# Four graph layers on one core: in the last layer TensorE reads the features in place, the first store is queued later, and the ending is cut in two

## The reference

```python
h = jnp.maximum(_layernorm(x, axis=-1), 0.0)
support = h @ weight
mask = (adj != 0)
rank = jnp.cumsum(mask, axis=1)
deg = rank[:, -1:]
k = jnp.minimum(deg, 100.0)
pos = rank - (deg - k)
w = mask * jnp.where(pos > 0, 0.5 ** (k - pos), 0.0)
x = x + w @ support + bias
```

## Time and profile before

| | before |
|---|---|
| median of 3 runs | 1181.51 us (1181.3 to 1183.08) |
| the profiled execution | 1179.22 us |
| its span in the profile | 1177.5 us |
| PE busy | 1082.3 us (92%) |
| DVE, ACT, POOL busy | 869.1, 769.3, 265.1 us |
| PE's mean granted clock | 0.956 of full speed |

### The profile page before, as it was taken

The page is one execution under the profiler, slowest core; times in us unless marked ns, Lnnn a source line. Parts: engine busy times, 40 slices in busy tenths (PEclk is TensorE's granted clock), DMA queues, the critical chain, the costliest instruction groups (busy, mean ns, idle before and its releaser), DMA issues.

```text
span 1177.5 us, 14630 instructions
## 1 busy us (share of the span) xinstructions
PE 1082.3 (92%) x5065; PEld 502.5 (43%) x5084; DVE 869.1 (74%) x927; ACT 769.3 (65%) x791; POOL 265.1 (23%) x183
## 2 busy tenths in 40 slices
PE   4899999996599999999898999999999999936987
PEld 1233333346533333333343545555555454534555
DVE  7999989965856666886689777767676777676543
ACT  3455555543566666866777798777778888535864
POOL 3110000000100000000143644333334444423533
PEclk9999999996889999999798999999999999967999
DMA  8999999950068888888344355545453554202652
GB/s 314 404 381 357 351 325 363 352 201 1 1 218 284 286 283 259 277 282 269 128 135 151 90 168 172 176 147 176 149 174 119 185 161 126 89 0 71 204 181 80
DMA packets 96301, 238.19 MB, mean 202 GB/s; under 512 B 16368, under 2 KB 45040, under 8 KB 79856
## 3 DMA queue, kind: packets, MB, share of 16 engines
q1 hardware_dynamic: 87024, 220.62, 56.4%
q10 hardware_dynamic: 9216, 16.78, 3.7%
HBM read 219.55 MB, written 17.83 MB: 202 GB/s over the span
## 4 chain that ended last, share of the span: by engine, by line
PE 75%; DVE 14%; issue 5%; ACT 5%; DMA 1%; POOL 1%; SPq 0%; DVEq 0%; ACTq 0%; POOLq 0%
PE PS L453 48%; PE PS L659 9%; PE PS L597 5%; PE PS L598 4%; PE PS L687 4%; DVE TB L1149 3%; PE PS L485 1%; PE PS L475 1%; ACT work L882 1%; PE PS L463 1%; PE PS L711 1%; ACT work L785 1%; DVE work L1428 1%; DVE work L1422 1%; ACT work L956 1%
## 5 line engine op out<-in xcount | busy, mean ns | idle before, releaser
L412 POOL TENSOR_TENSOR ring<-work,ring 128x1024 f32<-128x1024 f32 x58 | 139.2, 2400 | 474.7 <-DVE work L1428 474.7
L1275 DVE TENSOR_TENSOR work<-work,ring 128x1024 f32<-128x1024 f32 x128 | 151.2, 1222 | 75.3 <-ACT work L882 75.0
L819 ACT ACTIVATE work<-PS 128x1024 uint8<-128x1024 f32 x128 | 124.1, 1021 | 118.5 <-PE PS L453 118.5
L882 ACT ACTIVATE work<-PS,att_sc 128x1024 f32<-128x1024 f32 x128 | 147.7, 1202 | 78.6 <-PE PS L598 71.2
L453 PE MATMUL PS<-ring,work 128*65 128x256 f32 (+1 forms) x592 | 189.3, 467 | 6.4 <-DVE work L1452 2.8
L453 PE MATMUL PS<-work 128*64 128x512 f32 (+1 forms) x656 | 168.7, 559 | 0.1
L1422 DVE SCALAR_TENSOR_TENSOR work<-PS,work 128x1024 f32<-128x1024 f32 x72 | 88.1, 1223 | 90.6 <-PE PS L453 77.4
L659 PE MATMUL PS<-TB,TA 65*128 65x512 f32 x288 | 141.0, 612 | 3.5 <-DVE work L1422 3.5
L453 PEld LDWEIGHTS PS<-ring,work 128*65 128x65 f32 x592 | 80.4, 138 | 92.2 <-issue 69.1
L961 ACT ACTIVATE work<-work 128x1024 f32<-128x1024 f32 x72 | 76.0, 1055 | 43.7 <-DVE work L1422 43.6
L597 PE MATMUL PS<-work 128*128 128x512 f16 x256 | 99.0, 387 | 4.8 <-DVE work L1098 3.1
(11 more groups left out here) (211 smaller groups left out, 1511.5 us busy)
## 6 DMA issues: line engine op xcount, KB each, us to landing
ring<-in_adj_t SPq DMA_DIRECT2D x96, 1024.0 KB, 5.3
ring<-in_adj_t SPq DMA_DIRECT2D x103, 512.0 KB, 4.1
work<-in_adj_t SPq DMA_DIRECT2D x32, 1024.0 KB, 7.9
codes<-work ACTq DMA_DIRECT2D x64, 256.0 KB, 7.0
ring<-codes SPq DMA_DIRECT2D x64, 256.0 KB, 3.1
H<-in_adj_t SPq DMA_DIRECT2D x25, 512.0 KB, 4.0
X<-in_x SPq DMA_DIRECT2D x2, 512.0 KB, 5.2
out_x<-X SPq DMA_DIRECT2D x2, 512.0 KB, 4.4
```

What stands on the lines that cost most here:

```text
L412: nc.gpsimd.tensor_tensor(near(n), sums(n), near(n), ALU.mult).then_inc(sem("near_ready"), 1)
L819: nc.scalar.activation(made[:, k, u * UNIT:(u + 1) * UNIT], PS[:, (4 + 2 * u) * BANK:(6 + 2 * u) * BANK], ACT.Relu).then_inc(sem("codes_ma ...
L882: nc.scalar.activation(att[:, u, :], PS[:, (4 + 2 * u) * BANK:(6 + 2 * u) * BANK], ACT.Sigmoid, bias=att_sc[:, 2:3], scale=att_sc[:, 1:2]) ...
L1275: V.tensor_tensor(prob[:, m % 4, :], att[:, u, :], ring[:, s % RING, u * UNIT:(u + 1) * UNIT], ALU.mult)\
```

## The change

1. PE reads its stationary operand from `S3` itself. `sstage`, POOL's 64 copies and the semaphore `staged3` are gone. PE waits for `parts3_ready` 1 ahead of step 0 of each half's first group and for 2 ahead of step 16, where it waited for 2 ahead of the first.
2. As the address in `S3` differs in each step, PE's 56 looped steps are written out.
3. `store(0)` goes behind all loads of codes in SP's queue.
4. At the end ACT copies the first 512 columns of the sums and DVE the other 512; PE turns and DVE adds each part apart, and each is stored by a transfer of its own (`store_quarter`).

```diff
+            def store_quarter(a):
+                t = TG + a * TG // 2
+                sp.wait_ge(sem("quarter_ready"), a + 1)
+                sp.dma_start(out_nodes[:, t:t + TG // 2], X[:, t:t + TG // 2]).then_inc(sem("stored"), 16)
...
-                if h:
-                    store(0)
...
-            store(1)
-            sp.wait_ge(sem("stored"), 16 * G)
+            store(0)
+            for a in range(2):
+                store_quarter(a)
+            sp.wait_ge(sem("stored"), 16 * 3)
...
-            pool.wait_ge(sem("parts3_ready"), 1)
-            for h in range(2):
-                for k in range(4):
-                    if h:
-                        pool.wait_ge(sem("agg3_done"), h * T + k - 4 + 1)
-                    nc.gpsimd.tensor_copy(sstage[:, k, :].rearrange("p (s c) -> p s c", s=3), S3[:, k, :, :])\
-                      .then_inc(sem("staged3"), 1)
...
             def to_nodes(rhs, at, dst, b=None):
                 for a in range(2):
-                    if b is not None:
-                        bias_rows(b, dst + a)
-                    for q in range(4):
...
+                    ins = to_nodes_bank(rhs, at, dst, a, b)
+                return ins
+
+            def to_nodes_bank(rhs, at, dst, a, b=None):
...
-            pe.wait_ge(sem("parts3_ready"), G)
 
             def step3(h, s, k, first=False):
 
-                pe.wait_ge(sem("staged3"), s + 1)
+                if s in (0, TG):
+                    pe.wait_ge(sem("parts3_ready"), 1 + s // TG)
...
-                            ins = add(PS[D * c:D * c + D, b * BANK:(b + 1) * BANK], sstage[:, k, part * D:(part + 1) * D],
+                            ins = add(PS[D * c:D * c + D, b * BANK:(b + 1) * BANK], S3[:, s % T, part, :],
...
-                with pe.Fori(1, T // 4) as it:
-                    for k in range(4):
-                        step3(h, it * 4 + (h * T + k), k)
-            pe.wait_ge(sem("sums_out3_v"), 1)
-            to_nodes(ident[:, :], UNIT, 2).then_inc(sem("agg3_nodes"), 1)
+                for n in range(4, T):
+                    step3(h, h * T + n, n % 4)
+            for a in range(2):
+                pe.wait_ge(sem("sums_out3_v" if a else "sums_out3_a"), 1 if a else 2)
+                to_nodes_bank(ident[:, :], UNIT, 2, a).then_inc(sem("agg3_nodes"), 1)
...
+            one("sums_out3_a", TA[:, UNIT:UNIT + BANK], banks(6, 7), ACT.Copy, ("agg3_done", 2 * T))
...
-            copy_out("sums_out3_v", TA[:, UNIT:2 * UNIT], PS[:, 6 * BANK:8 * BANK], ("agg3_done", 2 * T))
-            result(1)
+            copy_out("sums_out3_v", TA[:, UNIT + BANK:2 * UNIT], banks(7, 8), ("agg3_done", 2 * T))
+            dve.wait_ge(sem("bias3_added"), G)
+            for a in range(2):
+                t = TG + a * TG // 2
+                dve.wait_ge(sem("agg3_nodes"), 2 + a)
+                V.tensor_tensor(X[:, t:t + TG // 2], X[:, t:t + TG // 2],
+                                banks(2 + a, 3 + a).rearrange("p (t c) -> p t c", c=D), ALU.add).then_inc(sem("quarter_ready"), 1)
```

More of the change, by code:

```diff
@@ L138, in graph_layers @@
         st = [sb(f"st{k}", [P, T]) for k in range(10)]
-        sstage = sb("sstage", [P, 4, 3 * D], BF16)
         kmask = sb("kmask", [P, 1])
@@ L431, in _ @@
                   .then_inc(sem("bias3_added"), 1)
-            pool.wait_ge(sem("parts3_ready"), 1)
-            for h in range(2):
-                for k in range(4):
-                    if h:
-                        pool.wait_ge(sem("agg3_done"), h * T + k - 4 + 1)
-                    nc.gpsimd.tensor_copy(sstage[:, k, :].rearrange("p (s c) -> p s c", s=3), S3[:, k, :, :])\
-                      .then_inc(sem("staged3"), 1)
-                pool.wait_ge(sem("parts3_ready"), G)
-                with pool.Fori(1, T // 4) as it:
-                    for k in range(4):
-                        pool.wait_ge(sem("agg3_done"), it * 4 + (h * T + k - 4 + 1))
-                        nc.gpsimd.tensor_copy(sstage[:, k, :].rearrange("p (s c) -> p s c", s=3), S3[:, it * 4 + k, :, :])\
-                          .then_inc(sem("staged3"), 1)
         @block.tensor
@@ L458, in to_nodes @@
                 for a in range(2):
-                    if b is not None:
-                        bias_rows(b, dst + a)
-                    for q in range(4):
-                        o = banks(dst + a, dst + a + 1).rearrange("p (r b c) -> p b r c", r=2, b=4)
-                        ins = mm(o[:, q, :, :], TA[:, at + a * BANK + q * P:at + a * BANK + (q + 1) * P], rhs,
-                                 start=b is None, stop=True, skip_group_check=True)
+                    ins = to_nodes_bank(rhs, at, dst, a, b)
+                return ins
+            def to_nodes_bank(rhs, at, dst, a, b=None):
+                if b is not None:
+                    bias_rows(b, dst + a)
+                for q in range(4):
+                    o = banks(dst + a, dst + a + 1).rearrange("p (r b c) -> p b r c", r=2, b=4)
+                    ins = mm(o[:, q, :, :], TA[:, at + a * BANK + q * P:at + a * BANK + (q + 1) * P], rhs,
+                             start=b is None, stop=True, skip_group_check=True)
                 return ins
```

## The result

| | before | after |
|---|---|---|
| median | 1182.3 us (1181.3 to 1183.83, 4 runs) | 1173.74 us (1173.37 to 1173.83, 4 runs) |
| ratio | | 0.9926 (0.9909 to 0.9943) |
| the profiled execution, its span | 1179.22, 1177.5 us | 1173.66, 1171.9 us |

The change made the kernel 8.6 us faster by the medians and 5.6 us by the profiled executions.

The account below looks back on a forecast made before the run. PE's matmul rate was taken to bound most of the fourth layer, with losses at start, turn and end. 1.0 + 2.95 + 2.3 = 6.25 us, with 0.65 for the clock, takes 1181.5 to 1174.6 us; range 1171.8 to 1178.0.

Parts of the forecast that it names:

- The start (1.0): Fourth layer's first steps: PE waits for one DVE sum, not two; 1.2 us earlier, some lost to half clock, gain 1.0.
- The turn (2.95): Between the halves in the fourth layer: PE's whole 2.95 us stall goes once the store no longer delays loads of codes.
- the cover: At the turn: power 40 is ready near 1131.5, PE needs it at 1134.40; 2.9 us of cover, so no new wait.
- Unrolling (0): PE's looped steps in the fourth layer: writing them out gains or costs 0 us, with 5 more code packets.
- Rival (e): PE's written-out steps: PE catches up with its own code and waits for packets; 17 us slower, 1198.6 us; chance 0.04.
- The end (2.3): After the last step: copies, turns and sums in halves give 1.2 us, bytes 1.2 less 0.1 for overlap; gain 2.3.
- The term of the bytes, 1.2 - 0.1: Last store: only 256 KB remains last, saving 1.2 us of byte time, less 0.1 where the two transfers meet.
- The last bytes flow for 2.4 us again: At the final stores: a sign that the prediction is wrong, byte flow still lasting 2.4 us.
- Rival (d): Final stores: the two are served one behind the other, end gains 0.5, total 5.1 us, 1176.4 us; chance 0.04.
- The clock's allowance (0.65): Turn of the halves: the stall may cost other executions a 1.3 us slow stretch; half, 0.65, added for the median.
- Rival (b): Clock doesn't fall ahead of the first steps, or fell mostly at the turn: gain 8.9 us, 1172.6 us; chance 0.14.
- theory C: From the experiments: the gain's rest is TensorE's clock, often falling in the kernel before's stall at the turn.

Follow-up runs that it names:

- after_again: The changed kernel timed once more, unaltered: ratio 0.9917 to the kernel before, mean 1173.0 us.
- unroll_only: The kernel before with only PE's 56 looped steps written out, POOL still staging: ratio 0.9986.
- store_only: The kernel before with only the first store moved behind the loads of codes: ratio 0.9970, mean 1177.3 us.
- one_store: The changed kernel with the last half stored by one 512 KB transfer after both sums: ratio 0.9938, mean 1175.5 us.
- direct_only: The kernel before with PE reading S3 itself, steps written out and the early start; store and ending as before: ratio 0.9980, mean 1179.2 us.
- store_in_place: The changed kernel with the first store put back between the loads: ratio 0.9962 to the kernel before, mean 1178.1 us.
- b_again: The kernel before timed once more, unaltered: ratio 1.0002.
- end_only: The kernel before with only the ending cut in two: ratio 0.9988, mean 1180.0 us.
- stall_busy: The changed kernel with the first store back between the loads and 12 unread matmuls in the resulting stall: ratio 0.9948, mean 1177.1 us.
- late_start: The changed kernel with PE waiting for both sums of the feature parts ahead of step 0: ratio 0.9942, mean 1175.8 us.

## Why the prediction was right, by its own steps

The sum of 6.25 us for the profiled execution came out: 6.24 from the first flip to the end with the same hold (`before` and `after_again`). The profile of the result showed 5.6, the 6.7 of the table less the 1.1 by which its flip was late; that both lie near 6.25 is partly chance. Term by term, with `after_again` for like and like:

| term | forecast | result's profile | `after_again` |
|---|---|---|---|
| start | 1.0 | 1.52 | 1.12 |
| turn | 2.95 | 3.15 | 3.15 |
| end | 2.3 | 2.01 | 1.96 |

**The start (1.0)** was on the path as said. The first sum gave 1.2, the pause behind the two sums shrank from 0.29 to 0.04, which I had left out though its row stood there, and 0.3 went back to the slow time, as worked out. The result's profile shows 0.4 more because its linear map was that much shorter, which comes with the early hold. What I missed is that with the late start the slow time can last longer: 49.63 and 49.76 us in two of the six profiles whose first step waits for both sums, 48.16 or 48.17 in the other four. The two are just those with the early hold, in which the linear map took 4.29 and 4.28 us and not 4.69 or 4.70. With the early start and idle PE it is 48.50 in all six, with either hold. Why the hold and the start decide it together stays open.

**The turn (2.95)** gave 3.15, and the cover held: with the store gone from between the loads, alone or with the rest, PE had no wait there.

**Unrolling (0)** is not told from nothing: the ratio of `unroll_only` (0.9971 to 1.0002) allows a gain of up to 3.4 us, but the rows leave no room for one. 28 steps take 36.40 us looped (`store_only`) and written out (`after`), the longest wait of the matmuls without a releaser is still 0.2 us after the change, and q8 has 4 packets more (5 estimated). Rival (e) falls.

**The end (2.3)** gave 2.0, but not in the way that I had said. Copies, turns and sums took as the rows of half the size said: 0.60, 2.07 and 0.69; that is the 1.2 us which remain when `one_store` is taken off. The term of the bytes, 1.2 - 0.1, had the mechanism wrong. I had the first quarter's bytes nearly through when the second's begin, so that 1.2 us of bytes are left. In fact the bytes begin 0.9 us after the issue of the first store (1167.71 to 1168.6; before, 1173.27 to 1174.2), which is when the second is issued, and then all 512 KB flow in one stream of 2.4 us. "The last bytes flow for 2.4 us again" was one of my signs of being wrong, and it came true. What the two transfers give is that the same stream starts earlier: 0.1 us behind the last sum's end at 1168.51, where it was 1.0 behind it before. That is worth the 0.83 us of `one_store`, near the estimated 1.1 by luck. From the last sum's end to the span's end it is 3.4 us, not 3.0. Rival (d) falls all the same, as it would have left 0.5.

**The clock's allowance (0.65)** was too small. Of six profiles with an idle stall at the turn three show the fall (`direct_only`, `store_in_place`, `unroll_only`; not `before`, `b_again`, `end_only`), at 1.65 to 1.7 us each: 0.85 on average, where I had 0.65. None of the eight others shows it. The longer slow time at the start is the other part, which I had not seen. With the early hold and the turn's 1.68 taken off, `unroll_only` takes 113.15 us from the first flip to the end and `after` 105.19: a gain of 7.96, where it is 6.24 with the late hold. By two of six executions with the early hold this estimate gives 6.24 + 0.57 + 0.85 = 7.7 us of the 8.6 that were measured. The rest, 0.9 us, is within the interval (6.7 to 10.8 us). So the gain of the median is two things: some 6.2 us of work and waits taken out of the chain, and some 1.4 us of clock losses that came with two of the idle times. Rival (b) had the clock's direction right but for another reason: ahead of the first steps it fell all the same.

Open: what of the spread comes from where. `store_only` has no stall and spreads over 5.0 us, `direct_only` has one and spreads over 3.1; the means of `stall_busy` and `store_in_place` point the way of theory C, but their intervals overlap. And six profiles give the share of executions only roughly.

## What to carry to other kernels

- A store or any other transfer that waits for a late result should stand in its queue behind the loads that don't; a load that could be issued some eleven microseconds early hides behind the steps only while nothing ahead of it in its queue waits. Here that was worth 3.1 us.
- Ask of each idle time of TensorE what its clock does behind it. The stall at the turn cost 3.1 us where the clock held and 4.4 to 5.0 where it fell, 1.7 of it by the clock, and the profiled execution can be of the luckier kind: compare mean granted clocks of several executions before a span is taken as the base of a sum, and compare profiles that agree ahead of the change.
- If an idle time can't be removed, matmuls that nobody reads can give back the clock's part: ahead of the first steps 13 of them gave 1.7 us in the profile.
- Cutting the last store in two lets its bytes start earlier; it did not halve the time in which they flow.

## What the runs showed of the hardware

- At the first steps the clock fell at full idle times of 4.97, 4.72 (`late_start`) and 3.50 us alike, and held (2.4 GHz, not 1.2) where 13 matmuls left 0.70 or 0.90 us idle. At the turn, 2.57 us idle in `direct_only` were followed by half clock and 2.95 in the kernel before were not: the length of the pause alone doesn't decide it.
- The times of 70 executions of the kernel before, on three chips, lay mostly in groups some 2 us apart, with the mean granted clock falling from 0.958 in the fastest to 0.949 in the slowest. That is a spread of 8.8 us, as large as the whole gain. The Trainium skill (TensorE: Matmul & The Clock Gate, What's actually happening) says that the moments at which the clock is decided are not tied to the kernel's start, so that one kernel ramps differently from run to run; the groups agree with it, and so do the two profiles of `before` and `b_again`, the same kernel with a mean granted clock of 0.83 and 0.87 between 280 and 360 us.
- A DVE operation with both operands in SBUF took 2.91 us beside POOL's product and 1.22 alone, and which of two it hit moved the fourth layer's start by 0.9 us. The Trainium skill (SBUF — State Buffer, Who interferes with whom) gives DVE and GpSimd a shared port pair that the first to come holds for its whole instruction; the rows agree (before, DVE's sum at 1030.93 began 0.02 us ahead of POOL's product and took 1.22; after, at 1031.12, it began 0.07 behind and took 2.91), but no run here took the port away to show it.
- Two 256 KB stores issued 0.8 us apart flowed as one stream of 2.4 to 2.5 us, like one store of 512 KB, at 217 and 218 GB/s. The first bytes came 0.9 us after the issue in both.
